# A graph network kernel on one core: scatters of edge rows spread over three stages, edge lists loaded during the attention, and half of the block sums narrowed from 168 to 104 columns

## The reference, cut to what matters

```
L0: agg[row] += deg^-1/2[row] * deg^-1/2[col] * h[col];  agg @ W.T + b
L1: attention over the edges, 4 heads of 32: softmax by destination of leaky_relu(q[src].k[dst]), times v[src]
L2: twice: agg[dst] += h[src] * edge_weight;  (agg + h) / (count + 1), two matrices, leaky relu;  then @ W_agg.T + b_agg
L3: xw = h @ W;  ew = edge_attr @ edge_w;  out[dst] += xw[src] * ew;  out + b
```

## Time and profile before

| what | value |
|---|---|
| median of three runs | 3131.64 us |
| the profiled execution: its own time | 3137.08 us |
| the profiled execution: span in the profile | 3135.3 us |
| busy: PE, DVE, POOL, ACT | 74%, 62%, 63%, 42% |
| mean granted TensorE clock | 0.875 |
| mean DMA rate | 91 GB/s |

### The profile page before, as it was taken

The page is one execution under the profiler, slowest core; times in us unless marked ns, Lnnn a source line. Parts: engine busy times, 40 slices in busy tenths (PEclk is TensorE's granted clock), DMA queues, the critical chain, the costliest instruction groups (busy, mean ns, idle before and its releaser), DMA issues. The chain is left out here.

```text
span 3135.3 us, 63975 instructions
## 1 busy us (share of the span) xinstructions
PE 2324.6 (74%) x22192; PEld 1705.1 (54%) x22192; DVE 1929.2 (62%) x3807; ACT 1301.7 (42%) x2282; POOL 1985.7 (63%) x1608
## 2 busy tenths in 40 slices
PE   3667677750039578787777788798993799999998
PEld 2466666640014245555555555553542587877776
DVE  7999999960023577777777777721112465656564
ACT  0466666650000377777777777500001222222221
POOL 2378878787772388788888888300000488887885
PEclk6799998875569679989999999999996799999998
DMA  6266666661146111111111111199692322222222
GB/s 77 95 168 188 185 185 180 186 186 15 11 99 160 59 48 46 42 45 42 45 45 45 45 44 41 39 228 221 140 213 9 66 55 61 55 56 55 54 56 56
DMA packets 219167, 285.61 MB, mean 91 GB/s; under 512 B 130289, under 2 KB 163960, under 8 KB 215725
## 3 DMA queue, kind: packets, MB, share of 16 engines
q1 hardware_dynamic: 170258, 246.53, 31.5%
q0 software_dynamic: 48720, 36.84, 6.2%
HBM read 171.50 MB, written 112.09 MB: 90 GB/s over the span
## 5 line engine op out<-in xcount | busy, mean ns | idle before, releaser
L385 POOL DMA_INDIRECT scratch_slots<-sort_pay,sort_slot x400 | 630.8, 1577 | 171.5 <-issue 171.2
L1796 POOL TENSOR_TENSOR score<-score,rise 125x500 f32<-125x500 f32 (+1 forms) x609 | 671.6, 1137 | 47.8 <-DVE peaks L1732 43.8
L2334 POOL DMA_INDIRECT gathered_rows<-scratch_projected,src_i x425 | 524.3, 1234 | 195.2 <-issue 194.6
L1732 DVE CUSTOM_DVE_ANT_0 score<-raw,log_in 125x500 f32<-125x500 f32 (+1 forms) x609 | 354.7, 619 | 151.9 <-PE raw L1617 87.8
L1679 ACT ACTIVATE rise<-raw 125x1000 f32<-125x1000 f32 (+1 forms) x350 | 314.3, 917 | 165.0 <-DVE peaks L1732 83.5
L1632 PE MATMUL probsT<-ident,score 125*125 125x125 f32 x2175 | 358.4, 294 | 29.8 <-ACT score L1688 13.1
L1632 PEld LDWEIGHTS probsT<-ident,score 125*125 125x125 f32 x2175 | 298.3, 200 | 106.8 <-DVE weighed L1753 67.0
L843 PE MATMUL built<-pair_weight,hot 125*128 125x125 bf16 x3750 | 265.5, 237 | 107.6 <-DVE pair_weight L790 107.6
L843 PEld LDWEIGHTS built<-pair_weight,hot 125*128 125x128 bf16 x3750 | 243.5, 107 | 123.7 <-DVE pair_weight L790 123.7
L790 DVE TENSOR_TENSOR pair_weight<-hot,w_parts 125x3840 bf16<-125x3840 bf16 x125 | 270.7, 2165 | 17.2
L1617 PE MATMUL raw<-QT,key 32*125 32x500 f32 (+1 forms) x1400 | 200.1, 642 | 93.3 <-DVE peaks L1732 90.2
(11 more groups left out here) (304 smaller groups left out, 4392.3 us busy)
## 6 DMA issues: line engine op xcount, KB each, us to landing
weights_in<-scratch_weightsT SPq DMA_DIRECT2D x50, 1093.8 KB
scratch_weightsT<-wT SPq DMA_DIRECT2D x25, 1367.2 KB
scratch_logs<-log SPq DMA_DIRECT2D x75, 437.5 KB
log_in<-scratch_logs SPq DMA_DIRECT2D x150, 218.8 KB
counts_in<-scratch_counts SPq DMA_DIRECT2D x25, 683.6 KB
scratch_counts<-cc SPq DMA_DIRECT2D x24, 683.6 KB
gathered_rows<-scratch_projected,src_i POOLq DMA_INDIRECT x425, 3.4
scratch_slots<-sort_pay,sort_slot POOLq DMA_INDIRECT x400
```

What stands on the lines that cost most here:

```text
L385: nc.gpsimd.indirect_dma_start(rows, bass.IndirectOffsetOnAxis(ap=sort["slot"][:, b, c:c + 1], axis=0), pay[:, c, :], None).then_inc(sort[ ...
L1732: nc.vector.tensor_tensor_reduce(out=score[u][h][:, at:at + w], in0=raw[:, h, 0:w], in1=log_in[:, at:at + w], scale=1.0, scalar=-3e38, op0 ...
L1796: nc.gpsimd.tensor_tensor(score[u][h][:, at:at + w], score[u][h][:, at:at + w], rise[:, b, h, 0:w], ALU.add).then_inc(added, 1)
L2334: nc.gpsimd.indirect_dma_start(gathered[:, g % GATHERS, k, :], None, projected, bass.IndirectOffsetOnAxis(ap=src_i[:, FIRST + g, k:k + 1], ...
```

## The change

**Scatters in three stages.** `PLACED_IN_ADJACENCY` is now 5: blocks 0 to 4 are placed in `adjacency`, block 5 in the first layer, and blocks 6 to 9 by a new POOL list in `weighted_layers`. The addresses and the packing buffers live longer, or are made anew in each stage.

**Lists loaded in the attention.** SP loads `base_i`, the unsorted half of `src_i` and `dst_i` and the nine copies of the edge matrix after the attention's last log load. `one_over_degree` gets a POOL list that clears `mix` and `quad_mix` and 15 semaphores of the irregular branch. The sorted half of `src_i` and `dst_i` (needed by `general_edges` alone) is loaded by SP at the end of the edge layer's loop.

**Narrow second chunk.** The chunk of ranks 128 to 255 is summed over the destinations 64 to 167 of its block, 104 and not 168; its `rel` is lowered by 64, and a third entry of `worst` sets `irregular` where that would be negative. `goals` becomes two instructions a round, of 2 x 168 and 2 x 104 elements.

```
-PLACED_IN_ADJACENCY = SORT_BLOCKS - 1
+REACHES = ((0, REACH), (64, REACH))
+GATHERED = SORTED // (EG * P)
+PLACED_IN_ADJACENCY = 5
+PLACED_IN_FIRST_LAYER = 1
+PLACED_EARLY = PLACED_IN_ADJACENCY + PLACED_IN_FIRST_LAYER
...
+def place_blocks(nc, T, pool, sort, slots, first, end):
+    nc.gpsimd.dma_start(sort["raw"][:], attribute_block(T, first)).then_inc(sort["raw_in"], 16)
+    for b in range(first, end):
+        place_block(nc, T, pool, sort, slots, b, end)
+    wait_placed(pool, sort, end)
...
             link(nc.vector.tensor_tensor(sort_dst[:], sort_dst[:], spread_ps[:].unsqueeze(2).broadcast_to([P, SORT_BLOCKS, COLS]),
                                          ALU.subtract))
-            nc.vector.tensor_copy(sort["rel"][:], sort_dst[:])
-            nc.vector.tensor_reduce(worst[:, 1:2], flat_of(sort_dst), axis=AX.X, op=ALU.max)
...
             link(nc.vector.tensor_scalar(rank[:], rank_ps[:], float(SLOT_ROWS), -1.0, ALU.min, ALU.add))
+            link(nc.vector.tensor_scalar(deep[:], rank[:], FULL - 0.5, None, ALU.is_ge))
+            nc.vector.tensor_reduce(worst[:, 1:2], flat_of(sort_dst), axis=AX.X, op=ALU.max)
+            link(nc.vector.scalar_tensor_tensor(sort_hi[:], deep[:], -float(REACHES[1][0]), sort_dst[:], ALU.mult, ALU.add))
+            nc.vector.tensor_copy(sort["rel"][:], sort_hi[:])
+            link(nc.vector.tensor_reduce(worst[:, 2:3], flat_of(sort_hi), axis=AX.X, op=ALU.min))
             nc.vector.tensor_scalar(worst[:, 0:1], worst[:, 0:1], SLOT_ROWS - 0.5, None, ALU.is_ge)
-            nc.vector.tensor_scalar(worst[:, 1:2], worst[:, 1:2], REACH - 0.5, None, ALU.is_ge).then_inc(judged, 1)
-            nc.vector.tensor_scalar(deep[:], rank[:], FULL - 0.5, -float(FULL * LISTS * 2 - 1), ALU.is_ge, ALU.mult)
+            nc.vector.tensor_scalar(worst[:, 1:2], worst[:, 1:2], REACH - 0.5, None, ALU.is_ge)
+            nc.vector.tensor_scalar(worst[:, 2:3], worst[:, 2:3], -0.5, None, ALU.is_lt).then_inc(judged, 1)
+            link(nc.vector.tensor_scalar(deep[:], deep[:], -float(FULL * LISTS * 2 - 1), None, ALU.mult))
...
 def regular_gcn_layer(nc, T, counts, X, H, W, ones, out_degree, sort, slots, used_before):
...
-            for b in range(PLACED_IN_ADJACENCY, SORT_BLOCKS):
-                place_block(nc, T, pool, sort, slots, b)
-            wait_placed(pool, sort, SORT_BLOCKS)
+            place_blocks(nc, T, pool, sort, slots, PLACED_IN_ADJACENCY, PLACED_EARLY)
...
+def fetch_last_layer(nc, T, sp, last):
+    with nc.allow_non_contiguous_dma(reason="runs of five edges, and one destination of every group"):
+        sp.dma_start(last["base_i"][:], T["dst"].rearrange("(o g r) -> o g r", o=1, r=EG * P)[:, :, 0]).then_inc(last["in"], 16)
+        for name, out in (("src", last["src_i"]), ("dst", last["dst_i"])):
+            sp.dma_start(out[:, GATHERED:, :], T[name][SORTED:].rearrange("(g p c) -> p g c", p=P, c=EG)).then_inc(last["in"], 16)
+    for k in range(EG):
+        sp.dma_start(last["mix"][k * EDIM:(k + 1) * EDIM, k, :], T["L3_gnn_edge_w"]).then_inc(last["in"], 16)
+    for k in range(4):
+        sp.dma_start(last["quad_mix"][k * SLOT:k * SLOT + EDIM, k, :], T["L3_gnn_edge_w"]).then_inc(last["in"], 16)
...
 def attention(...)
...
                 for g in range(GROUPS):
                     sp.wait_ge(summed, (TILES - 2) * (HEADS * GROUPS) + HEADS * (g + 1))
                     load_log(TILES - 1, g)
+            fetch_last_layer(nc, T, sp, last)
...
 def one_over_degree(...)
+        @block.gpsimd
+        def _(pool):
+            clear_used(pool, left)
+            nc.gpsimd.memset(last["mix"][:], 0.0)
+            nc.gpsimd.memset(last["quad_mix"][:], 0.0)
...
 def weighted_layers(...)
+        @block.gpsimd
+        def _(pool):
+            place_blocks(nc, T, pool, sort, slots, PLACED_EARLY, SORT_BLOCKS)
...
 def edge_layer(...), its preparation
-                nc.gpsimd.memset(mix[:], 0.0).then_inc(mix_zero, 1)
-                nc.gpsimd.memset(quad_mix[:], 0.0).then_inc(mix_zero, 1)
...
-                    sp.dma_start(base_i[:], T["dst"].rearrange("(o g r) -> o g r", o=1, r=EDGES)[:, :, 0]).then_inc(edges_in, 16)
-                    sp.dma_start(src_i[:], T["src"].rearrange("(g p c) -> p g c", p=P, c=EG)).then_inc(edges_in, 16)
-                    sp.dma_start(dst_i[:], T["dst"].rearrange("(g p c) -> p g c", p=P, c=EG)).then_inc(edges_in, 16)
-                sp.wait_ge(mix_zero, 2)
-                for k in range(EG):
-                    sp.dma_start(mix[k * EDIM:(k + 1) * EDIM, k, :], T["L3_gnn_edge_w"]).then_inc(attr_in, 16)
-                for k in range(QUAD):
-                    sp.dma_start(quad_mix[k * SLOT:k * SLOT + EDIM, k, :], T["L3_gnn_edge_w"]).then_inc(attr_in, 16)
...
-                dve.wait_ge(edges_in, 48)
+                dve.wait_ge(last["in"], 16 * LAST_LOADS)
                 nc.vector.tensor_copy(base_f[:], base_i[:]).then_inc(base_ready, 1)
-                link(nc.vector.tensor_copy(dst_rel[:], dst_i[:]))
+                link(nc.vector.tensor_copy(dst_rel[:, FIRST:], dst_i[:, FIRST:]))
...
 def edge_layer(...), its loop, at the end of SP's list
+                with nc.allow_non_contiguous_dma(reason="runs of five edges"):
+                    for name, out in (("src", src_i), ("dst", dst_i)):
+                        sp.dma_start(out[:, 0:GATHERED, :], T[name][0:SORTED].rearrange("(g p c) -> p g c", p=P, c=EG)
+                                     ).then_inc(last["in"], 16)
+                sp.wait_ge(last["in"], 16 * (LAST_LOADS + 2))
...
                     for c in range(QUAD):
-                        ins = nc.tensor.matmul(block_ps[:, 0:REACH], sent[:, r % 2, c, :], goal[:, r % 2, c, :],
+                        first, end = REACHES[c % 2]
+                        ins = nc.tensor.matmul(block_ps[:, first:end], sent[:, r % 2, c, :], goal[c % 2][:, r % 2, c // 2, :],
                                                start=(j == 0 and c == 0), stop=(j == PER_BLOCK - 1 and c == QUAD - 1))
...
-                    nc.vector.tensor_tensor(goal[:, r % 2], rel.unsqueeze(2).broadcast_to([FULL, QUAD, REACH]),
-                                            span[:].unsqueeze(1).broadcast_to([FULL, QUAD, REACH]),
-                                            ALU.is_equal).then_inc(s_goal, 1)
+                    for h, (first, end) in enumerate(REACHES):
+                        shape = [FULL, 2, end - first]
+                        nc.vector.tensor_tensor(goal[h][:, r % 2], rel.rearrange("p (s h) -> p s h", h=2)[:, :, h].unsqueeze(2)
+                                                .broadcast_to(shape), span[:, 0:end - first].unsqueeze(1).broadcast_to(shape),
+                                                ALU.is_equal).then_inc(s_goal, 1)
```

More of the change, by code:

```diff
@@ L657, in _ @@
             pe.wait_ge(judged, 1)
-            for k in range(2):
-                ins = nc.tensor.matmul(spread_ps[0:1, 0:1], worst[:, k:k + 1], ones[0:P, 0:1], start=(k == 0), stop=(k == 1))
+            for k in range(3):
+                ins = nc.tensor.matmul(spread_ps[0:1, 0:1], worst[:, k:k + 1], ones[0:P, 0:1], start=(k == 0), stop=(k == 2))
             ins.then_inc(judged_all, 1)
@@ L2111, in edge_layer @@
     QROWS = QUAD * SLOT
-    assert FIRST * EDGES == SORTED and LISTS % 2 == 0
+    assert FIRST * EDGES == SORTED and FIRST == GATHERED and LISTS % 2 == 0
+    base_i, src_i, dst_i, mix, quad_mix = [last[k] for k in ("base_i", "src_i", "dst_i", "mix", "quad_mix")]
     with ExitStack() as c:
@@ L2615, in program @@
                 "p (b c) -> p b c", c=COLS)
-            with ExitStack() as lists:
-                hold = lists.enter_context
-                keys = hold(sb("keys", [P, WINDOWS // GRP, 2, 2 * GRP, 2], BF16))
-                w_parts = hold(sb("w_parts", [P, WINDOWS // GRP, 3, 2 * GRP, 2], BF16))
-                steps = hold(sb("steps", [P, FULL], BF16))
-                used = window_starts(nc, T, table, starts, X, ident, ones, iota, iota_tile, irregular, sort)
-                used = edge_slots(nc, T, W, table, starts, X, H, norm, ident, keys, w_parts, steps, gathered, ones, irregular,
-                                  sort, slots, used)
-                used = adjacency(nc, T, counts, logs, weightsT, ident, keys, w_parts, steps, out_degree, in_parts, sort, slots, used)
@@ new lines, in program @@
+            w_parts = hold(sb("w_parts", [P, WINDOWS // GRP, 3, 2 * GRP, 2], BF16))
+            steps = hold(sb("steps", [P, FULL], BF16))
+            used = window_starts(nc, T, table, starts, X, ident, ones, iota, iota_tile, irregular, sort)
+            used = edge_slots(nc, T, W, table, starts, X, H, norm, ident, keys, w_parts, steps, gathered, ones, irregular,
+                              sort, slots, used)
+            used = adjacency(nc, T, counts, logs, weightsT, ident, keys, w_parts, steps, out_degree, in_parts, sort, slots, used)
@@ L2631, in program @@
+        with nc.If(nc.values_load(irregular[0:1, 0:1], min_val=0, max_val=1) != 0):
```

(9 more changed lines are left out.)

97 lines of the change are left out of this document (48 added, 49 removed).

## The result

The changed kernel takes 2907.91 us (median of four runs, 2899.49 to 2911.64); the kernel before, with one run more than was shown above, 3135.94 us. The ratio is 0.9272, 95% interval 0.923 to 0.9315. The prediction was 2908 us, the profiled execution to be 2913: it is 2911.64 us, its span 2909.9 us against 3135.3. By medians the gain was 228 us in the first pair and 214 in the third series (3126.65 to 2912.95). In the first series it was 157 us, on another chip: see the experiments.

A forecast was written before the change was run, and what follows sets the result against it. POOL alone was taken to hold the adjacency's end and to bound the edge loop, with list loads holding the preparation. Terms -194 + 1 + 14 - 46 + 2 - 1 = -224 us took 3131.64 to 2908; range 2881 to 2935.

The forecast's parts named there:

- Adjacency, -194: Adjacency's end: five blocks finish before SP's last store, whose landing then ends the block; -194 us (-190 to -196).
- Weighted layers, +14: Weighted layers' first step: scatters displace the weight stream, 9 to 19 us, middle taken; second step 0, POOL's blocks hidden.
- Free scatters: Rival in the weighted layers: small writes slip between weight packets, +14 becomes 0, total 2894 us; chance 0.15.
- rival of double cost: Weighted layers: small writes hold a full engine longer, about +33 us in place of +14, total 2927; chance 0.12.
- Preparation, -46: Edge layer's preparation: TensorE's 46.0 us wait goes because the lists already lie in SBUF; -46 us (-44 to -48).
- list loads at 0: Attention's end: SP's new list loads take 26 us, hidden with 45 us to spare before its next work; 0.
- sorting, +2: Sorting: about four more instructions on VectorE, which is the path there; +2 us (1 to 3).
- loads at the loop's end: End of the edge layer's loop: SP's two loads take 25 us, ending 12 us before the last sum; 0 (0 to +5).
- Loop, 0: Edge layer's loop: TensorE's 17 us saving and VectorE's 1.7 us cost lie beside POOL's gathers; 0 (-17 to +2).
- Both lie beside POOL's 1.54 us a gather: Loop's step: POOL paces it at 1.54 us a gather, so TensorE's and VectorE's changes don't show; 0.
- a test that I had written down: Sign of a wrong forecast: a loop shorter by over 5 us would mean POOL didn't set it.
- Attention: Attention stage: new loads follow its last log load and stay hidden; 0, or 26 us if uncovered.

The follow-up runs named there:

- first pair: The kernel before and the changed kernel as first measured and profiled: medians 3135.94 and 2907.91 us, ratio 0.9272.
- third series: Four kernels on a third chip, with the changed kernel and the kernel before both profiled: medians 2912.95 and 3126.65 us, ratio 0.934.
- first series: Four kernels on another chip, testing what shortened the gathers: changed kernel 3001.61 us beside 3158.29 for the kernel before, ratio 0.9527.
- nine_early: Changed kernel with placement undone: nine blocks in the adjacency, one in the first layer, none in the weighted layers; 3168.43 us, ratio 1.0016.
- four_left_out: Changed kernel with blocks 6 to 9 not placed at all in the weighted layers; a single run of 2993.74 us.
- late_one_goal: Changed kernel with one wide goal instruction, four wide sums, six blocks in adjacency, three in weighted layers after 24 weight slices; 2910.58 us.
- sums_twice: Changed kernel in which TensorE repeats the five sums of every gathered item, same result; median 2970.80 us.
- one_goal: Changed kernel with the narrow chunk undone: one goal instruction of 672 elements, all sums over 168 destinations; 2958.38 us, ratio 0.9373.
- wide_split: Changed kernel with both chunks summed over 168 destinations, goals still in two instructions of 336 elements; a single run of 2985.03 us.
- changed_again: The changed kernel unaltered, rerun as the first series' yardstick; 3001.61 us, ratio 0.9527.
- first profile: The changed kernel's first profiled execution, against the kernel before; 2911.64 us, its span 2909.9 us against 3135.3.
- three_narrow: Changed kernel with two of five gathers an item left out, narrow sums kept; a single run of 2852.03 us.

## Why the prediction was right, and where it was not

That the total was met within 2 us (-225.4 between the two spans, -224 predicted) is in part luck: the adjacency and the loop brought 6 and 9 us more than their terms, and the attention took 7 that no term had.

**Adjacency, -194.** Right in size and mechanism: -194.5 in the third series, and TensorE's wait in `nine_early` is 194.5 us longer too. In the first pair it was -200.2: counted from the start of the one-hots, SP's last store was issued at 572.8 us and before at 578.8. I had held SP's stores fixed, and they move by a few us.

**Weighted layers, +14.** Right in mechanism: `four_left_out` shows that the scatters cause it. In size it is 13 to 18 by three comparisons, inside 9 to 19, and 18 by the medians of all profiles; single profiles lie 10 to 30 apart, so the term is less sure than its hit suggests. The second step took 0 to 3 us more, where I had 0. The choice between bounds was lucky as to its reason (I took the middle); what the runs show is nearer to the upper one, the engine time. Free scatters are out. The rival of double cost (33) is beyond even the longest first step (187.0 us, 29 above the median without scatters). What the Trainium skill ("DMA: Bandwidth & Descriptors", section "Specifications") says of transfers under 512 bytes would speak for that rival; in this case it did not double the cost. One block beside the stream costs some 7 us (18 us for the 2.5 blocks of the first step, 8 for the one of `late_one_goal` against the 158.6 of `four_left_out`), 4 to 12 with the spread. POOL's pace there, 66 to 70 us from block to block, was right to 3 us.

**Preparation, -46; list loads at 0; sorting, +2.** -44 to -45, 0 and +2.3 to +2.7. SP had 40 us to spare at the attention's end, 45 predicted. The loads at the loop's end (issued 2859.16 to 2874) were over before SP's next work at 2900.87.

**Loop, 0.** The step that failed: "Both lie beside POOL's 1.54 us a gather". The gather's duration is not fixed; a long goal instruction of VectorE holds the gather that starts during it. Splitting the goals gave 4 to 10 us in the quiet pairs. My own figure had already been the mean over stretched ones (1.23 against 1.20 undisturbed). With it failed a test that I had written down, that a loop shorter by over 5 us would mean that POOL didn't set it: it was shorter by 9.7 and every gather still followed the last by 0.30 us. The sizes of the hidden work were right: 500 + 369 ns against 497 + 364, and 16.3 us of TensorE against 17.

**What no term held.** TensorE's distance to the bound. I had read 0.6 us of POOL's waits as safety; the distance was 35 us on a quiet run (`sums_twice`). When TensorE lost more than that, in the first two series, the loop took 73 us more (97 in `nine_early`) and the changed kernel's ratio went to 0.9527. The range did not hold 3001 us. Nor can I say why the narrow chunk cost 43 us there: TensorE's clock was low for longer (106 us against 65 in `one_goal`), but `wide_split`, with 68 us, was almost as slow. This stays open, as does the source of the late ends.

**Attention.** +4 to +7 where I had 0. Both profiles of the kernel before have it at 976 to 979 us up to the first product, the twelve of changed kernels at 980.5 to 998.7. By what I had put down for `changed_again`, this is then no difference between runs. The new loads don't explain it: they are issued 888 us after the first score, and 860 us after it, at the 650th of VectorE's 700 score instructions, the first profile was already 5 us behind. No run isolates what does.

## What to carry to other kernels

A scatter can be hidden under a stage that is full of DMA, but at the price of its engine time, not of its bytes: here some 7 us for 40 DMAs of 125 rows (4 to 12 with the spread between profiles), against some 60 us unhidden. Before calling work hidden beside a bound engine, ask how far the next engine is from the bound (leave some of the bound's work out, or double the other's), since that distance is what a bad run eats. And the duration of a GpSimd DMA issue is not a constant: look at its spread, and at what VectorE ran during the long ones.

## What the runs showed that I had not expected

- A gather that started during a 0.85-us VectorE instruction with two SBUF inputs was held until about its end and took up to 1.87 us instead of 1.20; one that had started before it was not. Two instructions of 0.50 and 0.37 us in its place reduced the slow gathers from 75 to 27.
- In the first profile's loop TensorE's granted clock fell to half after idle gaps of 0.8 to 3.1 us. In `changed_again` the 18 us after one of 1.5 us ran at 0.55 and 0.69. In `sums_twice` it fell without any gap, for 44 us. In `three_narrow`, which had no doubled sums and only two gaps over 0.5 us, the longest of 0.9, it stayed at 1.00. So the distance of 61 us that the full clock gives is not to be had: 35 us were measured.
- In two series of three, on two chips, TensorE's results were taken up late by an idle ScalarE: 20 to 34 of 84 copies, 1.4 to 1.9 us on average, and the loop was 33 to 97 us longer than in the first profile. It showed with five gathers an item and not with three, on the same chip.
